# A transformer block in one kernel: a down tile's PSUM bank, one V copy's place, and the order of the last batch's output shares

## The reference

```
x = x + 0.5 * ffn(layernorm(x))
x = x + attention(layernorm(x))
x = x + 0.5 * ffn(layernorm(x))
ffn(x)       = gelu(x @ w1 + b1) @ w2 + b2        # 256 -> 1024 -> 256, the same weights twice
attention(x) = softmax(q k^T / 8 + slope * -|i - j|, causal) @ v, 16 heads of 64, then @ w_out + b_out
```

## Time and profile before

| What | Value |
|---|---|
| median of 3 runs | 2169.64 us |
| the profiled execution's own time | 2169.53 us |
| its span, first to last instruction | 2167.7 us |
| TensorE busy | 2115.9 us, 98% |
| VectorE busy | 1525.4 us, 70% |
| ScalarE busy | 1272.0 us, 59% |
| GpSimd busy | 1143.1 us, 53% |
| mean granted TensorE clock | 0.996 |

### The profile page before, as it was taken

The page is one execution under the profiler, slowest core; times in us unless marked ns, Lnnn a source line. Parts: engine busy times, 40 slices in busy tenths (PEclk is TensorE's granted clock), DMA queues, the critical chain, the costliest instruction groups (busy, mean ns, idle before and its releaser), DMA issues.

```text
span 2167.7 us, 42138 instructions
## 1 busy us (share of the span) xinstructions
PE 2115.9 (98%) x14480; PEld 1715.6 (79%) x14480; DVE 1525.4 (70%) x4121; ACT 1272.0 (59%) x3156; POOL 1143.1 (53%) x1988
## 2 busy tenths in 40 slices
PE   7999999999999999999999999999999999999998
PEld 6687787877878788787886878878787787877867
DVE  6776767767676676767767677676766777667674
ACT  5756656466565665756557465674646646565572
POOL 2754636546474563745547365473654637445361
PEclk9999999999999999999999999999999999999999
DMA  3432515234152342524425143251533415234142
GB/s 132 132 84 81 144 32 144 78 94 122 45 142 69 107 109 54 145 56 117 108 62 139 45 136 90 69 149 28 145 83 94 128 40 146 69 103 113 45 132 59
DMA packets 130294, 209.70 MB, mean 97 GB/s; under 512 B 42192, under 2 KB 70960, under 8 KB 130080
## 3 DMA queue, kind: packets, MB, share of 16 engines
q1 hardware_dynamic: 97888, 143.86, 23.6%
q0 software_dynamic: 25952, 58.38, 10.7%
q10 hardware_dynamic: 6240, 4.76, 0.8%
HBM read 14.95 MB, written 8.39 MB: 11 GB/s over the span
## 4 chain that ended last, share of the span: by engine, by line
PE 57%; DVE 19%; ACT 8%; issue 6%; POOL 4%; ACTq 3%; SPq 1%; DMA 1%; POOLq 0%; DVEq 0%
PE ps L361 56%; DVE P L937 5%; DVE gl L828 4%; ACT P L705 3%; ACTq L301 3%; DVE gh L896 2%; DVE xs L860 2%; POOL P L1126 2%; POOL PT L290 2%; DVE x L876 1%; DVE st L836 1%; SPq L290 1%; POOL rstd L1112 1%; ACT qk L651 1%; DVE xs L866 1%
## 5 line engine op out<-in xcount | busy, mean ns | idle before, releaser
L705 ACT ACTIVATE P<-P,mx 128x512 f32<-128x512 f32 (+3 forms) x1024 | 563.4, 553 | 281.6 <-DVE mx L929 281.4
L1126 POOL TENSOR_SCALAR P<-P,rs 128x512 f32<-128x512 f32 (+3 forms) x1024 | 539.2, 544 | 227.3 <-DVE rs L920 224.0
L290 POOL DMA_DIRECT2D PT<-P x646 | 324.1, 507 | 384.0 <-DVE P L937 361.1
L937 DVE STREAM_TRANSPOSE P<-P 128x1792 f32<-128x1792 f32 (+1 forms) x256 | 372.5, 1484 | 24.7 <-POOL P L1126 24.7
L361 PE MATMUL ps<-qk 64*128 64x512 f32 (+3 forms) x2048 | 321.3, 443 | 2.4 <-ACT qk L651 0.7
L361 PE MATMUL ps<-PT,v 128*64 128x256 f32 (+1 forms) x3072 | 306.7, 349 | 10.3 <-DMA PT<-P 8.7
L361 PE MATMUL ps<-w2h,gh 128*128 128x256 f32 x1024 | 291.9, 285 | 1.6 <-DVE gl L828 1.6
L361 PEld LDWEIGHTS ps<-PT,v 128*64 128x64 f32 x3072 | 204.3, 137 | 108.0 <-issue 17.1
L361 PE MATMUL ps<-w2l,gh 128*128 128x256 f32 x1024 | 289.7, 283 | 0.0
L361 PE MATMUL ps<-w2h,gl 128*128 128x256 f32 x1024 | 289.5, 283 | 0.0
L929 DVE CUSTOM_DVE_ANT_0 P<-ps,dist 128x512 f32<-128x512 f32 x256 | 166.1, 686 | 167.3 <-PE ps L361 166.8
(11 more groups left out here) (91 smaller groups left out, 4357.8 us busy)
## 6 DMA issues: line engine op xcount, KB each, us to landing
PT<-P SPq DMA_DIRECT2D x1392, 80.0 KB, 2.6
PT<-P POOLq DMA_DIRECT2D x646, 80.0 KB, 2.7
x<-in_L_attn_x SPq DMA_DIRECT2D x16, 512.0 KB, 4.4
out_y<-x SPq DMA_DIRECT2D x15, 512.0 KB, 2.9
xt<-xs SPq DMA_DIRECT2D x195, 32.0 KB, 2.0
xt<-xs POOLq DMA_DIRECT2D x165, 32.0 KB, 1.9
xt<-xs ACTq DMA_DIRECT2D x120, 32.0 KB, 2.2
raw<-in_L_ffn_w SPq DMA_DIRECT2D x2, 512.0 KB, 5.7
```

The costliest lines, as they stand in the source:

```text
L290: e.dma_start(PT[c % 2][32 * m:32 * m + 32, g, :], P[c % 3][32 * g:32 * g + 32, m, :]).then_inc(landed.sem, 16)
L705: e.activation(p, p, ACT.Exp, bias=mx[:, r, i:i + 1], scale=-1.0, accum_out=sm[:, r, i:i + 1]).then_inc(s_ex.sem, 1)
L937: e.transpose(p, p).then_inc(s_tr.sem, 1)
L1126: e.tensor_scalar(p, p, rs[:, 2 * (c % 2) + h, i:i + 1], 1.0, ALU.mult, ALU.mult).then_inc(s_nz.sem, 1)
```

## The change

There are five edits.

- In `begin`, the first down tile is asked for among (6, 7) and no longer among (5,).
- ScalarE copies the first V tile of step 6 before the exponentials of block row 2, and no longer after them, in every batch.
- In the last batch, TensorE does output shares 0 and 1 before `values(b, 5)`, and shares 2 and 3 after it; before, it did `values(b, 5)` and then shares 0 to 3. The four output tiles stand in banks 0, 1, 6, 7 and no longer in 0 to 3; the P times V products after them are asked for among 2 to 5 and no longer among 4 to 7.
- ScalarE makes the high parts of shares 0 and 1 ahead of `out_copy(b, 4)` and the exponentials of pair 7, and shares 2 and 3 where 0 and 1 were; VectorE makes the low parts of 0 and 1 ahead of the biased tiles of pair 7, and 2 and 3 where 0 and 1 were.
- The last LN transposes are asked for among (2, 3) and no longer among (6, 7).

```diff
@@ tensor, begin
                     up(2, b - 1, range(NM))
-                    among[0] = (5,)
+                    among[0] = (6, 7)
                     dn(2, b - 1, 0)
                 among[0] = (6, 7)
                 scores(b, 1)
@@ tensor, attention
-                    values(b, c - 2)
+                    if more or c < NC - 1:
+                        values(b, c - 2)
...
                 else:
-                    among[0] = range(4)
-                    for c in range(4):
-                        out_part(c, range(NT))
-                    among[0] = range(4, 8)
+                    among[0] = (0, 1, 6, 7)
+                    turn[0] = 7
+                    out_part(0, range(NT))
+                    out_part(1, range(NT))
+                    among[0] = range(2, 6)
+                    values(b, NC - 3)
+                    out_part(2, range(NT))
+                    out_part(3, range(NT))
                     values(b, NC - 2)
@@ tensor, after the loop
-            among[0] = (6, 7)
+            among[0] = (2, 3)
             ln_transpose(3, NB - 1, 0)
@@ scalar, attention
                 for c in range(2, NC):
+                    if not more and c == NC - 1:
+                        out_part_hi(0)
+                        out_part_hi(1)
                     if c >= 3:
                         out_copy(b, c - 3)
...
-                    exps(b, c, 2)
+                    if c != NC - 2:
+                        exps(b, c, 2)
                     for tile in steps_v(b, c)[:1]:
                         proj_copy(b, tile)
+                    if c == NC - 2:
+                        exps(b, c, 2)
                     exps(b, c, 0)
...
                 else:
-                    for c in range(2):
+                    for c in (2, 3):
                         out_part_hi(c)
                     spread(e, b, NC - 2, LAST_ACT, s_la[NC - 2])
-                    for c in range(2, 5):
-                        out_part_hi(c)
+                    out_part_hi(4)
                     out_copy(b, NC - 3)
@@ vector, attention
                 for c in range(2, NC):
+                    if not more and c == NC - 1:
+                        out_part_lo(0)
+                        out_part_lo(1)
...
                 else:
-                    out_part_lo(0)
-                    out_part_lo(1)
+                    out_part_lo(2)
+                    out_part_lo(3)
                 turned(b, NC - 1, 1)
...
                 if not more:
-                    for c in range(2, NC):
+                    for c in range(4, NC):
                         out_part_lo(c)
```

## The result

The changed kernel takes 2211.12 us (median of four runs, 2209.33 to 2216.39) against 2170.64 for the kernel before: ratio 1.0187, interval 1.0163 to 1.0211. It is slower by 40 us; 2198 was forecast, with 2183 to 2212 as the range. The profiled execution is the slowest of the four, 2216.39 with a span of 2214.6, which is 46.9 above the span before. Its mean granted clock is 0.982; the three others have 0.984 and 0.985.

The account below looks back on a forecast made before the run. TensorE, busy 2115.9 of 2167.7 us, was taken to bound the kernel. Terms -11.9 + 29.1 (step 6) + 10.7 (clock) + 0.7 (last batch) = +28.6 us on 2169.53 gave 2198, range 2183 to 2212.

Parts of the forecast that it names:

- case A: New wait of `values(b,4)` on the LN low half, clock falling in about half the batches: 2192 to 2204, chance 0.48.
- rival C: Clock falls at nearly every new wait, 14 x 1.53 us: 2208.8; chance 0.16 together with a second way near it.
- its neighbour: At the batch's start another wait replaces the 11.9 us gain: 2210; chance 0.16 together with rival C.
- scores of pair 1: Start of each batch after the first: the wait for bank 5 goes, 15 x 0.79 = 11.9 us off.
- from the second V tile to `values(b,4)`: Step 6: later start of `values(b,4)` loses 21.5 us in odd batches, 12.0 in even ones, 0.6 in batch 0.
- given back before P times V of pair 6: Before `values(b,6)`: old waits for P-transpose DMAs vanish, 5.0 of 5.8 us taken back, bounds 0 and 7.
- half clock in `values(b,4)` and `scores(b,7)`: After the new idle stretches the clock falls 7 times, 10.7 us lost, between 0 and 21.4.
- last batch: Idle 2.90 us before `values(15,5)` moves to about 4 us before `values(15,6)`; 0.7 us lost, bounds 2.9 gained, 2.5 lost.
- The bank exchange: Batches 1 to 14: `values(b,4)` gets bank 6, finds LN unit 0 there, and waits for VectorE's LN low half.
- The two prices of the wait: `values(b,4)` starts 3.07 us later in odd batches and 1.71 later in even ones, 7 times each.
- My row: Last batch before: idle 2.90 us, then clock 0.50; 24 P times V matmuls took 3.91 us against 2.38, 1.53 more.

Follow-up runs that it names:

- restored turn: Changed kernel with the bank counter set before P times V of pair 4 in batches 1 to 14, so it takes bank 7, not 6: 2161.83 us, ratio 0.9956.
- bank edit alone: Kernel before with only the first down tile asked for among banks 6 and 7 instead of 5: 2200.40 us, ratio 1.0135.

## Why the prediction was right, and what was mis-sized

Right in direction, in mechanism and in place; the time lies inside the range, but only 0.9 us under its upper end, and the profiled execution, 2216.4, lies above it. That much is luck. The forecast, case A, was 13 us too low, and what happened is nearly rival C, to which the text gave 0.16 with its neighbour. By the terms of the sum, from the two profiled executions, each stage measured from start to start and summed over the batches:

| Term | Forecast | Measured |
|---|---|---|
| scores of pair 1, 15 batches | -11.9 | -12.05 |
| from the second V tile to `values(b,4)`, batches 0 to 14 | +34.1 | +34.0 |
| given back before P times V of pair 6 | -5.0 | -2.9 |
| half clock in `values(b,4)` and `scores(b,7)` | +10.7 | +27.2 |
| last batch | +0.7 | +1.0 |
| sum | +28.6 | +47.2 (spans: +46.9) |

The first edit: right, and the runs with it in place keep all of it. The bank exchange, counted out from the order of the bank uses, is right: 14 waits, 3.00 and 2.53 us. That it is the bank and not the moved copy is shown by the restored turn. The two prices of the wait came from adding rows of one chain, and hit it to 0.1 us, because every link stood in the trace of before.

Given back: 2.1 us too much. I took most of the 5.8 us of waits for landings to vanish (and set the bound at 7, more than there was). In batches 3, 8 and 13 they do (2.4 us); the other three stand in batch 0, which the new wait does not reach, and stay.

The clock is the term that was mis-sized, twice. The count: 12 falls and not 7. I had taken only the stretches of 2.9 us or more, and the even batches, with 2.53, fell seven times out of seven. There four transposes stand between 0.78 and 2.53 us of idle time; I had counted only the idle time after them. The price: 27.2 / 12 = 2.3 us each instead of 1.53, 1.6 in five of them and 2.6 to 2.9 in seven (in batch 7 the product took 4.46 from start to start for 2.31, and the scores 3.01 for 2.36). My row was a case in which the clock rose again within the product. It bounded one fall, not the longest. Both bounds I had named (14 falls, 1.53 each, 21.4) were thus under what was measured, and the range held the time only because its end was set past rival C, and because the other executions lost less to the clock than the profiled one.

The last batch: right to 0.3 us, with the hole moved as forecast. The run of the last batch's edits alone adds that the delay of VectorE isn't what makes the second hole: with most of it gone the wait for the landing is 3.90 (3.69 in the changed kernel). That TensorE simply has its shares done early, while the spread of pair 6 still stands behind pair 7's biased tiles, is read from the program's order and not tested.

The Trainium skill (TensorE: Matmul & The Clock Gate, "HAM oscillation — how this bites in real kernels") tells of a loop in which a wait in every turn lets the clock fall in every turn. Its waits, about 3 to 5 us, are mostly longer than these. By the count the trace comes nearer to it than to my 7: the clock fell at 12 of the 14 waits.

## What to carry to other kernels

With a round-robin over PSUM banks, moving one use out of the rotation or into it exchanges the banks of everything up to the next reset; list who holds each bank after the edit, and look for the use whose predecessor is read out last. Where TensorE is the bound, a new wait of 2.5 to 3 us cost its length and, where the clock fell, 1.6 to 2.9 us more in half-speed products behind it. Filling the wait with products that nothing uses brought back the half-speed part, not the wait.

## What the runs showed of the hardware that was not expected

A stretch of 3.00 us idle behind the transposes was followed by a lower clock in five batches out of seven, with the same work around it, and one of 2.06 us in two out of seven. So the length of the idle time does not settle it, and the loss differs from one execution to the next: the changed kernel took 2209 to 2216 us, with mean clocks of 0.985 to 0.982, in the same order.

The longest idle time alone does not put the cases in order. The time in which TensorE does no product, transposes included, does. This is from the last product before step 6's transposes to the first behind them, one profiled execution each:

| Kernel, batches | Without a product, us | Longest idle in it | Clock fell |
|---|---|---|---|
| restored turn, odd | 1.85 | 0.82 | 0 of 7 |
| restored turn, even | 2.39 | 0.78 | 0 of 7 |
| before, even | 2.73 | 1.48 | 0 of 7 |
| bank edit alone, odd | 3.09 | 2.06 | 2 of 7 |
| changed, odd | 4.04 | 3.00 | 5 of 7 |
| changed, even | 4.57 | 2.53 | 7 of 7 |
| bank edit alone, even | 4.90 | 2.35 | 7 of 7 |

With ten products put into the stretch of 4.04 us (and of 4.57 in the even batches) it fell in none of 14. No run changes the transposes alone, so what they by themselves do to the clock is not shown.
